# Readout by transposes that add up in PSUM, and the input products of a unit made twice, in a Mamba block between two FFNs

## The reference

```python
def step(h, inp):                       # h: [B, 512, 16]
    dA_t, dB_t, x_t, C_t, t = inp
    h = h * dA_t + dB_t * x_t[:, :, None]
    nrm = jnp.sqrt(jnp.sum(h * h, axis=(1, 2), keepdims=True))
    fac = jnp.minimum(20.0 / (nrm + 1e-08), 1.0)
    h = jnp.where(t % 10 == 0, h * fac, h)
    y = jnp.einsum('bdn,bn->bd', h, C_t) + D_param * x_t
    return (h, y)
```

## Time and profile before

| | |
|---|---|
| Time, median of 3 runs | 1543.17 us (1541.73 to 1543.39) |
| Span of the profiled execution | 1540.7 us; its own time is not listed apart from those of the runs |
| PE, PEld, DVE, ACT, POOL busy | 95%, 66%, 82%, 73%, 61% of the span |
| Mean granted TensorE clock | 0.995 |
| DMA | 236.3 MB, 153 GB/s |
| Pre stage, scan's units, post stage | about 0 to 434 us, 434 to 1328 us, from there to the end |

### The profile page before, as it was taken

One profiled execution on the slowest core, in us unless ns is written; L12 is line 12 of the kernel. 1 busy time (PEld: TensorE's weight loads), 2 busy tenths in 40 slices (PEclk: granted clock), 3 DMA queues, 4 the chain that ended last, 5 costly groups with the idle time before them and its releaser, 6 DMA issues.

```text
span 1540.7 us, 25357 instructions
## 1 busy us (share of the span) xinstructions
PE 1463.5 (95%) x6854; PEld 1017.9 (66%) x6854; DVE 1256.0 (82%) x2526; ACT 1122.5 (73%) x2618; POOL 934.8 (61%) x956
## 2 busy tenths in 40 slices
PE   6999999999989999999999999999999998999998
PEld 5555555555456777777777777777666665677776
DVE  7775566646468999999999999999999998788885
ACT  4454455445999999999999999999999964233243
POOL 0223313321359999999999999999999997400000
PEclk9999999999999999999999999999999999999999
DMA  8225437443757666656656666565544448466420
GB/s 268 82 64 161 133 98 208 129 146 109 241 147 204 177 165 179 172 162 184 170 154 185 172 169 184 156 174 167 139 110 109 99 102 227 119 210 198 147 86 28
DMA packets 231429, 236.27 MB, mean 153 GB/s; under 512 B 45913, under 2 KB 197145, under 8 KB 231289
## 3 DMA queue, kind: packets, MB, share of 16 engines
q1 hardware_dynamic: 230344, 233.34, 53.3%
q10 hardware_dynamic: 944, 1.31, 0.2%
HBM read 136.31 MB, written 98.56 MB: 152 GB/s over the span
## 4 chain that ended last, share of the span: by engine, by line
DVE 35%; POOL 13%; PE 11%; issue 6%; DMA 2%; DVEq 1%; POOLq 1%; SPq 0%; ACT 0%; ACTq 0%
DVE h L1343 22%; POOL rc L1107 13%; DVE banks L1333 8%; PE banks L1492 3%; PE banks L1513 3%; PE banks L1523 3%; DVE qs L1327 2%; DVEq L1341 1%; PE banks L1167 1%; DMA ub<-scratch_ub 1%; DMA q_xc<-scratch_xc 1%; DVE q_ln_st L1769 1%; DVE q_g L1678 1%; POOLq L1115 1%; DVE q_x L1650 1%
## 5 line engine op out<-in xcount | busy, mean ns | idle before, releaser
L1343 DVE TENSOR_TENSOR_SCAN h<-decay,banks 128x352 f32<-128x352 f32 x820 | 710.4, 882 | 57.6 <-DVE banks L1333 2.9
L1118 POOL TENSOR_TENSOR hc<-h,bc 128x640 f32<-128x640 f32 x410 | 592.7, 1446 | 0.0
L1167 PE MATMUL banks<-hc,w_ident 128*128 128x320 f32 (+1 forms) x1664 | 525.7, 439 | 0.1
L1236 ACT ACTIVATE tb<-dtc,a 128x320 f32<-128x320 f32 (+1 forms) x832 | 417.4, 556 | 4.8 <-DVE x L610 4.8
L1167 PEld LDWEIGHTS banks<-hc,w_ident 128*128 128x128 f32 x1664 | 284.4, 191 | 70.3 <-issue 0.4
L1258 ACT ACTIVATE decay<-tb 128x640 f32<-128x640 f32 x410 | 295.1, 723 | 0.0
L1107 POOL TENSOR_TENSOR rc<-qs,w_mhalf 128x1 f32<-128x1 f32 x410 | 224.9, 549 | 111.0 <-DVE qs L1327 111.0
L1153 PE MATMUL banks<-ub 128*128 128x176 f32 x1640 | 273.0, 289 | 2.9 <-DMA ub<-scratch_ub 2.9
L1146 PEld LDWEIGHTS banks<-sc_ss,sc_ones 128*128 128x128 f32 x820 | 123.2, 189 | 158.5 <-ACT sc_sq L1247 153.1
L1153 PEld LDWEIGHTS banks<-ub 128*128 128x128 f32 x1640 | 217.1, 193 | 3.1 <-DMA ub<-scratch_ub 3.0
L1146 PE MATMUL banks<-sc_ss,sc_ones 128*128 128x1 f32 x820 | 151.6, 254 | 37.8 <-ACT sc_sq L1247 20.3
(11 more groups left out here) (133 smaller groups left out, 1764.9 us busy)
## 6 DMA issues: line engine op xcount, KB each, us to landing
ub<-scratch_ub SPq DMA_DIRECT2D x410, 107.5 KB
bc<-scratch_blk SPq DMA_DIRECT2D x205, 160.0 KB, 3.5
scratch_ub<-turned SPq DMA_DIRECT2D x64, 512.0 KB, 3.8
scratch_ub<-spread SPq DMA_DIRECT2D x64, 176.0 KB, 3.0
scratch_xc<-xc SPq DMA_DIRECT2D x8, 1024.0 KB, 4.8
scratch_sg<-sg SPq DMA_DIRECT2D x8, 1024.0 KB, 5.9
piece<-scratch_u SPq DMA_DIRECT2D x32, 256.0 KB, 3.8
q_ys<-scratch_y SPq DMA_DIRECT2D x8, 1024.0 KB, 5.7
```

The lines of the kernel that those rows point to most:

```text
L1118: pool.tensor_tensor(hc[:, pl % 2, :, at * S:(at + 1) * S] .rearrange("p (c b n) e -> p c b n e", c=KE, b=B)[:, :, b], state(m)[:, :, 0:S] ...
L1167: mm = pe.matmul(banks[:, y_bank(p), 0:KE * B * wide], w.ident[:], rhs, start=(n == 0), stop=(n == N - 1))
L1236: act.activation(tanh_rows(c, r), dtc[:, c % 2, k * B:(k + 1) * B, 0:blocks_of(c) * S].rearrange("p b (k e) -> p k b e", e=S), ACT.Tanh, s ...
L1343: dve.tensor_tensor_scan(state(m).rearrange("p r e -> p (r e)")[:, half], decay[:, m % DRING, half], psI[m % B][:, half], 0.0, ALU.mult, A ...
```

## The change

The readout is turned round. `hc` becomes one ring of RT = 80 times, laid out as [16 states, 80 times, 8 rows of channel group and batch]. For each group of GT = 16 times (128 groups) and each state, the 16 x 8 = 128 columns of `hc` are the weights of a transpose with the identity as moving operand, with `is_transpose=True`, `start` at the first state and `stop` at the last: 16 transposes add up into 128 columns of PSUM, with (time, row) on the partitions. PE makes TURNS = 5 of them a unit, from unit LAG = 5 on. A pair is 32 times, a quad now two pairs (four groups, one bank; banks 2 and 5 take turns). `summed_at(q)` is the unit in which quad q is complete. ACT copies each half of the quad to `yt` one and two units later, PE turns it back with four transposes three units later, and ACT copies the two pairs to `yc` four and five units later. SP stores 128 times at once, 16 stores.

POOL's `weigh` writes `hc` with the times 8 elements apart. From unit 2 * LAG = 10 on, `inputs` makes the four products twice, with the same operands into the same place; the count `inp_ready` comes after the eighth. The first projection moves to the last three units, two halves of it stand behind the sums of the last but one group, and the last group's sums and the last turn back come after it. `yt` ([128, 4, 128]) is a new buffer.

```diff
-QB = 4
-QUADS = (NB - 1) // QB + 1
-CQ = CB // QB
+GT = 16
+RT = math.lcm(S, GT)
+GROUPS = L // GT
+PAIRS = GROUPS // 2
+PT = 2 * GT
+QUADS = PAIRS // 2
+CP = 4
+YCHUNKS = PAIRS // CP
+TURNS = 5
+FILL = 320
+LAG = 5
...
+def blocks_in(g):
+    return (g * GT + GT - 1) // S + 1
+def summed_at(q):
+    return LAG + (4 * N * (q + 1) - 1) // TURNS
+def y_bank(q):
+    return 5 if q % 2 else 2
...
-    hc = second.put("hc", [P, 2, ROWS, QB * S])
+    hc = second.put("hc", [P, N, RT, KE * B])
...
         def weigh(m):
             j, b = m // B, m % B
-            pl, at = quad_of(j)
+            at = j * S % RT
...
-            if b == 0 and at == 0 and pl >= 2:
-                pool.wait_ge(y_summed, pl - 1)
+            if b == 0 and j * S >= RT:
+                pool.wait_ge(y_summed, (j * S + S - 1 - RT) // GT + 1)
             pool.tensor_tensor(
-                hc[:, pl % 2, :, at * S:(at + 1) * S]
-                .rearrange("p (c b n) e -> p c b n e", c=KE, b=B)[:, :, b],
+                hc[:, :, at:at + S, b::B].rearrange("p n t c -> p c n t"),
...
         def inputs(m):
             pe.wait_ge(ub_in[m % URING], 16 * (m // URING + 1))
-            for c in range(KE):
+            for c in [*range(KE if m >= 2 * LAG else 0), *range(KE)]:
...
-        def readout(p, n0, n1):
...
+        def sum_turned(k0, k1):
+            for k in range(k0, min(k1, GROUPS * N)):
+                g, n = divmod(k, N)
+                if n == 0:
+                    pe.wait_ge(hc_ready, blocks_in(g) * B)
+                    if g % 4 == 0 and g >= 8:
+                        pe.wait_ge(y_copied, g // 2 - 2)
+                lhs = hc[:, n, g * GT % RT:g * GT % RT + GT, :].rearrange("p t r -> p (t r)")
+                mm = pe.matmul(psG[y_bank(g // 4)][:, g % 4, :], lhs, w.ident[:], is_transpose=True, start=(n == 0), stop=(n == N - 1))
+                if n == N - 1:
+                    mm.then_inc(y_summed, 1)
+        def turn_back(q):
+            pe.wait_ge(yt_copied, 2 * q + 2)
+            for x in range(4):
+                mm = pe.transpose(psG[y_bank(q)][:, x, :], yt[:, x, :], w.ident[:])
+            mm.then_inc(y_turned, 1)
+        def project_first(x0, x1):
+            for x in range(x0, x1):
+                if x == 0:
+                    pe.wait_ge(ut_lo, halves(PIECES))
+                    pe.wait_ge(y_copied, PAIRS - 2)
+                post.project(pe, 0, x // 2, x % 2 * KE // 2, (x % 2 + 1) * KE // 2)
...
+        backs = {summed_at(q) + 3: q for q in range(QUADS)}
...
-            if m >= UNITS - 6:
...
-                readout(p, part * each, (part + 1) * each)
-            if m < QB * B + B:
+            if m >= UNITS - 3:
+                project_first((m - UNITS + 3) * 2, (m - UNITS + 4) * 2)
+            if m >= LAG:
+                sum_turned((m - LAG) * TURNS, (m - LAG + 1) * TURNS)
+            if m in backs:
+                turn_back(backs[m])
+            if m < 2 * LAG:
                 keep_busy(2 if m < B else 1)
...
-        readout(QUADS - 1, 0, N)
+        sum_turned((UNITS - LAG) * TURNS, (GROUPS - 1) * N)
+        project_first(6, 2 * G)
+        sum_turned((GROUPS - 1) * N, GROUPS * N)
+        turn_back(QUADS - 1)
...
+        def copy_yt(q):
+            act.wait_ge(y_summed, 2 * q + 2 if q % 2 else 2 * q + 4)
...
+            act.activation(yt[:, half, :], psG[y_bank(q // 2)][:, half, :], ACT.Copy).then_inc(yt_copied, 1)
+        def copy_y(q):
...
+            act.wait_ge(y_turned, q // 2 + 1)
+            act.activation(yc[:, c % 2, :, o:o + PT], psY[y_bank(q // 2)][:, q % 2 * PT:(q % 2 + 1) * PT, :].rearrange("p t r -> p r t"),
                            ACT.Copy).then_inc(y_copied, 1)
...
+        sums = {summed_at(q // 2) + 1 + q % 2: q for q in range(PAIRS - 2)}
+        turns = {summed_at(q // 2) + 4 + q % 2: q for q in range(PAIRS - 2)}
...
+            if m in sums:
+                copy_yt(sums[m])
+            if m in turns:
+                copy_y(turns[m])
```

More of the change, by code:

```diff
@@ L722 @@
 ROW = E + N * W
-LAST_EVEN = (UNITS - 6 - B) // (QB * B) - 2
-assert LAST_EVEN % 2 == 0 and (NB - 1) % QB == 0
+assert L % (CP * PT) == 0 and TT % (CP * PT) == 0
 Scan = namedtuple("Scan", """sync gpsimd tensor scalar vector load_first load_units tanhs decay_rates decay_scale masks
@@ L751, in halves @@
     return k if k < B else 2 * k - B
[L754 to L777, removed]
+def blocks_in(g):
[4 more added lines that the diff above has]
+    return 5 if q % 2 else 2
+assert all(LAG + N * g // TURNS >= blocks_in(g) * B for g in range(GROUPS))
 def scan_stage(nc, dram, w, areas, banks, sem, pre):
@@ L812, in scan_stage @@
     h = second.put("h", [P, 2, B, NCH, W])
-    hc = second.put("hc", [P, 2, ROWS, QB * S])
+    hc = second.put("hc", [P, N, RT, KE * B])
     assert second.offset <= pre.dt_place
-    yc = second.put("yc", [P, 2, KE * B, CT])
+    yc = second.put("yc", [P, 2, KE * B, CP * PT])
     piece.append(second.put("piece1", [P, KE, P]))
     turned.append(second.put("turned1", [P, 2, E], F32R))
+    yt = second.put("yt", [P, 4, P])
     EDGE = COLS - 2 * N * W
@@ L821, in scan_stage @@
     psT, psQ = banks[:, 3], banks[:, 4]
+    psY = {q: banks[:, q].rearrange("p (t r) -> p t r", r=KE * B) for q in (2, 5)}
+    psG = {q: banks[:, q].rearrange("p (g d) -> p g d", d=P) for q in (2, 5)}
     a_in, s_in, blk_out, consts = sem("a_in"), sem("s_in"), sem("blk_out"), sem("s_consts")
@@ L1033, in sync, with store_y @@
     def sync(sp, pre, post):
[L1034 to L1038, removed]
+        def store_y(c):
+            sp.wait_ge(y_copied, (c + 1) * CP)
+            sp.dma_start(dram["y"][:, :, c * CP * PT:(c + 1) * CP * PT], yc[:, c % 2]).then_inc(y_out[c % 2], 16)
         QP = piece_unit(B + 1) // B
@@ L1053, in sync @@
             dt_at[free(x0 + 1, 1)] = (c, 1)
-        for c in range(CHUNKS):
-            if c * CB + CB + QB + 2 < NB:
-                x0 = free(c * CB + CB + QB + 2, 2)
+        for c in range(YCHUNKS):
+            at = summed_at(2 * c + 1) // B + 4
+            if at + 2 * QP < NB:
+                x0 = free(at, 2)
                 y_at[x0 + QP if x0 in dt_at else x0] = c
@@ L1088, in sync @@
             if j in y_at:
-                store_y(y_at[j], CQ)
+                store_y(y_at[j])
             if dc == DCHUNKS - 1 and dk in (3, 5, 6, 8, 10, 11, 13, 14):
@@ L1093, in sync @@
                 post.fetch(sp, dk // 10, {3: "y", 5: "xc", 6: "sg", 8: "r", 10: "y", 11: "xc", 13: "sg", 14: "r"}[dk])
[L1094 to L1097, removed]
+        for c in range(len(y_at), YCHUNKS):
+            store_y(c)
     def gpsimd(pool):
@@ L1172, in keep_busy @@
         def keep_busy(times):
             for _ in range(times):
-                pe.matmul(banks[:, 5, 0:KE * B * QB * S], w.ident[:], w.s1[:, 0, 0:KE * B * QB * S].bitcast(F32),
-                          start=True, stop=True)
+                pe.matmul(banks[:, 5, 0:FILL], w.ident[:], w.s1[:, 0, 0:FILL].bitcast(F32), start=True, stop=True)
         pieces = {piece_unit(k): k for k in range(B, PIECES)}
-        each = N // (QB * B)
+        backs = {summed_at(q) + 3: q for q in range(QUADS)}
@@ L1308, in scalar @@
                     decays(n)
-            p, late = divmod(m - QB * B - B, QB * B)
-            if p >= 0 and late == (1 if p <= LAST_EVEN else 0):
-                copy_y(p)
+            if m in sums:
+                copy_yt(sums[m])
+            if m in turns:
+                copy_y(turns[m])
             if m - UNITS + 16 in (0, 3, 6, 9):
@@ L1319, in scalar @@
                     copy_low(act, pieces[m - 8 - x], psT, x * E // 2, (x + 1) * E // 2)
-        for p in range(QUADS - 2, QUADS):
-            copy_y(p)
+        for x in range(2):
+            copy_yt(PAIRS - 2 + x)
+        for x in range(2):
+            copy_y(PAIRS - 2 + x)
     def vector(dve, pre, post):
@@ L1543, in tensor @@
         turn_xn(0)
-        pe.wait_ge(scan.y_copied, QUADS)
+        pe.wait_ge(scan.y_copied, PAIRS)
         up(0, 0, 1)
```

28 lines of the change are left out of this document (10 added, 18 removed).

## The result

The changed kernel takes **1563.75 us** (median of 4 runs, 1561.68 to 1566.58) against 1542.45 for the kernel before in the same session: ratio 1.0139, 95% interval 1.0124 to 1.0154, so 21 us slower. The forecast was 1557.0, the range 1541 to 1620.

What follows compares the result with a forecast made beforehand. The prediction took the DVE and POOL chain of waits, 2.13 us a unit, as the bound. Turns back 7.8, collisions 7.9 and stutters -1.6 made 14.1 us on 1543.2, so 1557 us, range 1541 to 1620.

Steps and rivals of the forecast that it cites:

- the room of the square: Scan loop: how late ACT's square may come unpaid; doubled products cut it from 0.23 us to 0.04.
- The collisions: 36 scan units where ACT's copy of y meets a piece's copy: 0.22 us each, 7.9 us.
- The turns back: 31 loop units where PE turns a quad back with four transposes: 7.8 us lost in all.
- PE's sum of 2.33 us: PE's work in a unit with four transposes of a quad: 2.33 us against 2.13, 0.20 over.
- Copies with no piece's copy beside them: A 256-element ACT copy alone in a scan unit: 0.26 us, hidden in ACT's idle time, costing nothing.
- The stutters: 20 late carries of 0.08 us in the earlier kernel's loop go with the copies that made them: -1.6 us.
- The strides: POOL's strided write and ACT's strided PSUM read: taken as 0; rival, POOL slowed, 1742 us, chance 0.13.
- The clock: Rival, chance 0.11: transposes lower TensorE's clock in the scan; a tenth of 400 units slow gives +52 us, 1609.
- at the low level it would be busy throughout: Argument against the falling clock in the scan: PE would have no idle time at the low level.
- The tail: From the last sum on: less PE work but later projections, together 0, within 1.5 us either way.

## Why the prediction was right, and where it was not

**The direction and the first mechanism held.** The step that the forecast stood on, "the room of the square falls from 0.23 us to between 0.01 and 0.1; I take 0.04", came out at 0.07: the eight products end where it put them, and the next carry follows 0.11 us later. The spread copies show by undoing it that this is a cause.

**The collisions** were put at 36 x 0.22 = 7.9 us. 33 fell on units 25 to 390, for 6.1 us: 29 of them lengthened, by 0.21 each. Against the same units of the kernel before it is 5.2.

**The turns back** were put at 7.8 us and came to 3.0. The step that failed is PE's sum of 2.33 us for such a unit. It took 0.25 for the sum of squares up to the first product and 0.12 a transpose; when PE's queue is full the chains show 0.12 and 0.11. So the unit holds 0.12 + 0.97 + 5 x 0.11 + 4 x 0.11 = 2.08 us and fits in 2.13: the seven clean turns back cost nothing. With a subtraction (0.29) it is 2.37, 0.24 over; the eight measured 0.23 each, not 0.43. With two transposes of a piece it is 2.30, 0.17 over; the four measured 0.13, not 0.38.

**Copies with no piece's copy beside them** were put at nothing, hidden in ACT's idle time. In units with subtraction, transposes or nothing of a piece 14 are lengthened, by 3.7 us in all, but little of it is shown to be the copies'. Four of the 14 (33, 97, 289, 353; 1.4 us) are as long in the kernel before. Four more (139, 203, 267, 331; 1.2 us) are of the five late carries that come with the doubled products; in the kernel with the copies spread they take 2.42 to 2.43 us as well, three of them with no copy of y. About 1 us is left for the copies, so "nothing" was nearly right. The late carries are a cost of the doubling that the forecast doesn't have.

**The stutters** were to give back 1.6 us. The kernel before has 25 lengthened units between 25 and 390, 3.7 us: the six that both kernels share (2.1) and 19 stutters (1.6, as forecast). Four units with a piece's copy alone are lengthened in the changed kernel too (0.8), so the term was near 0.8. Lengthened units are then 13.6 - 3.7 = 9.9 of the 11.4 us; the other 1.5 are spread over units under 2.17, some 4 ns each, and no run says why.

**The number was near by some luck.** The forecast's 14.1 stood against 11.4 in the loop: the turns back were 4.8 us too dear. Outside the loop's middle the sum had nothing, and there the trace has 5.6 us in the last units, 1.6 in the first 25 and 1.4 in the tail. Of the measured 21 us the forecast's mechanism explains about half.

**The strides** cost what was taken for POOL, nearly nothing: 1446 ns became 1470 with a step of 32 bytes between the elements written, and the copy that reads PSUM with that step (L1286, 365 ns) is as long as the dense one (L1277, 362 ns). The Trainium skill, "GPSIMD Engine Reference", section 7, gives half more an element for SBUF reads with a step over 8 bytes; the write that stands here shows under 2%, and no run has POOL read that way.

**The clock** was a rival with 0.11, as a share of all units. It came true in another shape. In the loop the doubled products held 1.00; with single ones it was 0.86 and the kernel slower still. At the end it fell, in eleven units. The argument against the rival, "at the low level it would be busy throughout", was right and no comfort: PE was busy throughout for 24 us at 0.50 and the clock stayed there. The tail, "Together 0, within 1.5 us either way", covered what lies behind the last carry (+1.4); what was missing is a term for the last units of the loop, where the low clock follows a wait for `ub` that the kernel before has too, and where eight products at that clock make PE the bound. The wait's length doesn't decide it: with the copies spread PE waits 0.43 and 0.67 us for `ub` and the clock falls at 1299, while with ordinary sums and single inputs it waits 2.34 us and the clock stays at 1.00:

```profile
1299.18 0.69 PE L1152 MATMUL banks<-ub 128*128 128x176 f32 x4 [2.34 <-DMA ub<-scratch_ub]
```

The two kernels with ordinary sums there, or with single products there, show that it takes both. The first 25 units give another +1.6 us, with a granted clock of 0.82 over 434 to 460 us (0.93 before); their share wasn't tested by itself.

The Trainium skill, "TensorE: Matmul & The Clock Gate", Part 4, says that the full clock doesn't engage for transposes, which don't count as PE-busy in the same way. This case gives both answers. For it: single products and transposes 0.86, single products and ordinary sums 1.00, and at the end of the stage 0.50 with transposes against 1.00 with ordinary sums. Against it: the five idle transposes brought the clock from 0.57 to 1.00 and held it. Ordinary sums also keep PE busier (584 of 600 us against 495), so the first pair doesn't part the two causes; in the pair at the end PE was busy for 24.00 and 23.44 of 24 us, and busy time doesn't explain it. **What stays open** is what the chip counts: no run here says why transposes raised the clock in one place and a PE full of transposes and doubled products didn't in another.

## What to carry to other kernels

Before work is added to an engine that isn't the bound, work out from a clean unit how late each of its inputs may come, and list the units in which something else falls due as well: most of the 11 us came from such units, and moving the copies and the turns back took back 7 of them. Work that holds the clock up has a price at the low clock, where it takes twice as long: put it where a stall behind it can't turn it into the bound, and end it before the stage's last transfers. And take a change apart by its parts before it is judged: single products made the changed kernel slower by 26 us in units 25 to 392 (37.6 over the kernel before, not 11.4) and faster by 7 us in the last 17.

## What the runs showed of the hardware that was not expected

- Sixteen fp32 transposes that add up in one PSUM bank run at 0.11 us each at full clock (5 in 0.55 us in the chain) and 0.21 at the low one (5 in 1.07), as those of the turn back do (4 in 0.85 at the low one); adding up costs nothing. The ordinary fp32 sum of the same tile is two instructions, ten for five sums in 1.11 us in the chain.
- With single products and transposes the granted clock went up and down between the levels of 1.2 and 2.4 GHz through the whole loop, 0.86 on average over 600 to 1200 us; it fell and rose many times in one run, though PE (products and weight loads together) never idled for more than 1.23 us in that stretch.
- Five idle transposes a unit took a stretch from 0.56 to 1.00 and its units from 2.29 to 2.14 us on average.
- PE busy throughout from 1304 to 1338 us at 0.50 didn't bring the clock back in that time; most of the last eleven units took 3.13 us.
